# Rows of C by DMA instead of TensorE and ScalarE, and a rectifier moved from VectorE to ScalarE

## What is computed

```python
xz = x @ Win.T;  xi, z = xz[..., :256], silu(xz[..., 256:])
Bm, C = x @ WB.T, x @ WC.T                      # 16 values a token each
dt = softplus(x @ Wdt.T + bdt + dt_bias)
denom = 1 - dt * A * 0.5                        # A = -exp(A_log), 256 x 16
state[e, s] = (1 + dt*A*0.5) / denom * state[e, s] + dt / denom * Bm[s] * xi[e]
out[e] = sum_s state[e, s] * C[s]
y = layernorm(out * z) @ Wout.T
```

## Time and profile before

| | |
|---|---|
| median of 3 runs | 2897.46 us (2897.29 to 2911.29) |
| the profiled run | 2903.22 us, its span 2901.3 us |
| busy over the span | PE 2358.4 us (81%), DVE 1983.2 (68%), ACT 1950.0 (67%), POOL 1471.6 (51%) |
| state-space stage, 1279 to 2010 us | PE 509.56 us, DVE 658.89, ACT 538.78, POOL 538.20 of 731 |
| DVE in 40 slices | 2333367767767677458988989897776676767664 |
| DMA | 30.41 MB in the span, 3.5% of 16 engines |

### The profile page before, as it was taken

One profiled execution on the slowest core, in us unless ns is written; L12 is line 12 of the kernel. 1 busy time (PEld: TensorE's weight loads), 2 busy tenths in 40 slices (PEclk: granted clock), 3 DMA queues, 4 the chain that ended last, 5 costly groups with the idle time before them and its releaser, 6 DMA issues. The chain is left out here.

```text
span 2901.3 us, 47111 instructions
## 1 busy us (share of the span) xinstructions
PE 2358.4 (81%) x13516; PEld 1233.4 (43%) x13516; DVE 1983.2 (68%) x5318; ACT 1950.0 (67%) x4833; POOL 1471.6 (51%) x1308
## 2 busy tenths in 40 slices
PE   6999778888888888766766767776888888888887
PEld 3555445545555455422222222222454445544543
DVE  2333367767767677458988989897776676767664
ACT  3444357777777777567877677775777777776674
POOL 1222145545545555347776777774654554554442
PEclk9999879999999999978988888879999999999999
DMA  3000000000000000000000000000000000000000
GB/s 126 1 0 0 1 12 12 12 8 11 12 9 16 8 11 11 4 0 0 1 1 1 0 1 0 1 0 4 12 12 9 12 12 8 16 12 19 15 11 15
DMA packets 12195, 30.41 MB, mean 10 GB/s; under 512 B 2240, under 2 KB 2240, under 8 KB 11456
## 3 DMA queue, kind: packets, MB, share of 16 engines
q1 hardware_dynamic: 11968, 27.99, 3.5%
HBM read 9.11 MB, written 2.10 MB: 4 GB/s over the span
## 5 line engine op out<-in xcount | busy, mean ns | idle before, releaser
L500 POOL TENSOR_TENSOR arena<-arena 128x512 f32<-128x512 f32 x256 | 325.1, 1270 | 782.9 <-DVE arena L1469 782.9
L544 POOL TENSOR_TENSOR arena<-arena 128x512 f32<-128x512 f32 x256 | 328.8, 1301 | 128.5 <-ACT arena L1243 120.4
L1111 ACT ACTIVATE arena<-psum 128x512 f32<-128x512 f32 x256 | 152.6, 596 | 300.9 <-PE psum L824 300.5
L1475 DVE TENSOR_REDUCE SS<-arena 128x8 f32<-128x512 f32 x256 | 174.8, 683 | 259.3 <-ACT arena L1111 257.9
L824 PE MATMUL psum<-rest,HA 128*128 128x512 f32 x512 | 276.5, 623 | 51.1 <-DVE arena L1469 51.1
L513 POOL TENSOR_TENSOR P<-P,RS 128x512 f32<-128x512 f32 x256 | 266.5, 1041 | 93.8 <-DVE RS L1401 92.6
L1555 DVE TENSOR_TENSOR_SCAN arena<-arena,psum 128x512 f32<-128x512 f32 x256 | 310.9, 1215 | 3.2
L910 PE MATMUL psum<-BS,tabs 96*128 96x512 bf16 x384 | 146.7, 443 | 204.2 <-DVE arena L1555 202.4
L979 PE MATMUL psum<-arena,first 128*128 128x512 f32 x512 | 289.7, 655 | 10.9 <-POOL arena L535 10.6
L775 PE MATMUL psum<-HN,rest 128*128 128x512 f32 (+1 forms) x384 | 214.9, 674 | 98.9 <-ACT arena L1126 51.4
L506 POOL TENSOR_TENSOR arena<-arena,SC 128x512 f32<-128x512 f32 x256 | 273.1, 1067 | 29.8 <-DVE SC L1480 29.6
(11 more groups left out here) (222 smaller groups left out, 5878.9 us busy)
## 6 DMA issues: line engine op xcount, KB each, us to landing
arena<-arena SPq DMA_DIRECT2D x128, 128.0 KB, 2.3
rest<-in_rest SPq DMA_DIRECT2D x1, 4183.0 KB, 23.0
X<-in_x SPq DMA_DIRECT2D x1, 2048.0 KB, 11.0
out<-X SPq DMA_DIRECT2D x8, 256.0 KB, 2.4
first<-in_first SPq DMA_DIRECT2D x1, 1445.5 KB, 6.6
tabs<-in_tabs SPq DMA_DIRECT2D x1, 1216.0 KB, 13.5
```

The source lines that it names most:

```text
L500: nc.gpsimd.tensor_tensor(CQ[:, n % 2, :], CQ[:, n % 2, :], SQN[:, n % 2, :], ALU.add).then_inc(f_rope, 1)
L544: nc.gpsimd.tensor_tensor(WU[:, k % DEEP, :], RG[:, k % DEEP, :], U[t.j % 2][:, k % 2, :], ALU.mult).then_inc(m_wu, 1)
```

## The change

- The rows of C no longer go through TensorE and ACT. ACT copies the 32 rows of B and C from PSUM to a tile CF in SBUF (two deep) and rounds BS from CF. SP stores C's 16 rows of CF to DRAM (`c_rows`), waits for it, and loads each row back, repeated over 128 partitions, into CS, which is now four rows deep. A load waits for POOL's odd product four states back (`m_pco`); one semaphore for each of the four slots tells DVE and POOL that the row is there.
- DVE's even product reads CS instead of C_BANK; POOL's odd product reads CS as before.
- `spread_c` on TensorE and `copy_c` on ACT go.
- The positive part of v (PV) is made by ACT as a Relu with the bias, each half right behind its absolute value and ahead of the exponential, instead of by DVE.
- The first remainder (L1613) reads CF instead of SIDE; TensorE's later use of SIDE waits for CF.

```diff
@@ -283,20 +283,23 @@
         AB = shared("mamba", [128, DEEP, NT])
         WU = shared("mamba", [128, DEEP, NT])
         HS = shared("mamba", [128, DEEP, NT])
-        CS = shared("mamba", [128, 2, NT])
+        CS = shared("mamba", [128, 4, NT])
+        CF = [shared("mamba", [32, NT]) for k in range(2)]
         PC = shared("mamba", [128, DEEP, NT])
-        B_BANK, C_BANK, ACC_BANK = (bank[0], bank[2]), (bank[1], bank[3]), (bank[4], bank[5])
+        B_BANK, ACC_BANK = (bank[0], bank[2]), (bank[4], bank[5])
         SIDE = bank[6]
         STEPS = 2 * NS
-        m_bc = sem("m_bc")
+        m_cf = sem("m_cf")
+        m_cr = sem("m_cr")
+        c_rows = nc.dram_tensor("c_rows", (2, NS, NT), f32).ap()
-        m_cs = sem("m_cs")
+        m_cs = [sem(f"m_cs{k}") for k in range(4)]
@@ -471,8 +474,17 @@
                     k.wait_pair(f_x, -1)
                     sp_.dma_start(out[:, k.tokens(-1)], X[:, k.tokens(-1)]).then_inc(out_done, 16)
 
-            for ph in range(2):
-                passes(sp_, ph, sp_slot)
+            passes(sp_, 0, sp_slot)
+            for j in range(PAIRS):
+                for s in range(NS):
+                    if s == 0:
+                        sp_.wait_ge(m_cf, j + 1)
+                        sp_.dma_start(c_rows[j % 2, :, :], CF[j % 2][NS:2 * NS, :]).then_inc(m_cr, 16)
+                        sp_.wait_ge(m_cr, 16 * j + 16)
+                    if NS * j + s >= 4:
+                        sp_.wait_ge(m_pco, NS * j + s - 3)
+                    sp_.dma_start(CS[:, s % 4, :], c_rows[j % 2, s:s + 1, :].to_broadcast([128, NT])).then_inc(m_cs[s % 4], 16)
+            passes(sp_, 1, sp_slot)
             sp_.wait_ge(out_done, 16 * PAIRS)
 
 
@@ -529,10 +541,10 @@
             layers_pool(0)
             def odd_times_c(t, s):
                 k = 2 * s + 1
-                t.wait_ge(m_cs, NS, s + 1)
+                t.wait_ge(m_cs[s % 4], 64, 16 * (s // 4) + 16)
                 t.wait_ge(m_hs, STEPS, k + 1)
                 t.wait_ge(m_acc, STEPS, k + 1 - DEEP)
-                nc.gpsimd.tensor_tensor(PC[:, k % DEEP, :], HS[:, k % DEEP, :], CS[:, s % 2, :], ALU.mult).then_inc(m_pco, 1)
+                nc.gpsimd.tensor_tensor(PC[:, k % DEEP, :], HS[:, k % DEEP, :], CS[:, s % 4, :], ALU.mult).then_inc(m_pco, 1)
 
             def pool_turn(t):
                 for k in range(STEPS):
@@ -916,10 +928,6 @@
                     t.wait_ge(m_bs, 3, 3)
                 spread(t, k, k // 2, B_BANK[k % 2], m_bb)
 
-            def spread_c(t, s):
-                t.wait_ge(m_pce, NS, s - 1)
-                spread(t, s, NS + s, C_BANK[s % 2], m_bc)
-
             def half_sum(k, weight, source, done):
                 last = mm(STAT, weight(k), source[:, k, :], start=k == 0, stop=k == 1)
                 if k:
@@ -970,6 +978,7 @@
                 elif k in (20, 23):
                     half = (k - 20) // 3
                     t.wait_ge(m_zs if half else m_bd, 2, 1, pair=1)
+                    t.wait_ge(m_cf, 1, 1, pair=1)
                     mm(SIDE, W("b_win", 256 + 128 * half, 384 + 128 * half), HN[:, :], start=True, stop=True).then_inc(m_zp, 1)
 
             def accumulate(t, k):
@@ -984,15 +993,11 @@
             def pe_turn(t):
                 if t.states:
                     spread_b(t, 0)
-                    spread_c(t, 0)
                     spread_b(t, 1)
-                    spread_c(t, 1)
                 for k in range(STEPS):
                     if t.states:
                         if k + 2 < STEPS:
                             spread_b(t, k + 2)
-                        if k % 2 == 0 and 2 <= k < STEPS - 2:
-                            spread_c(t, k // 2 + 1)
                     if t.before:
                         pe_ending(t, k)
                     if t.after:
@@ -1198,6 +1203,7 @@
                     for half in range(2):
                         t.wait_ge(m_vp, 2, half + 1, pair=1)
                         A(AV[:, half, :], (SIDE, STAT)[half], ACT.Abs, bias=dt_bias_b[:, half:half + 1]).then_inc(m_abs, 1)
+                        A(PV[:, half, :], (SIDE, STAT)[half], ACT.Relu, bias=dt_bias_b[:, half:half + 1]).then_inc(m_max, 1)
                     t.wait_ge(m_abs, 2, 2, pair=1)
                     A(AV[:, :, :], AV[:, :, :], ACT.Exp, scale=-1.0).then_inc(m_exp, 1)
                     t.wait_ge(m_w, 1, 1, pair=1)
@@ -1210,8 +1216,10 @@
                 elif k == 21:
                     t.wait_ge(m_bp, 1, 1, pair=1)
                     t.wait_ge(m_bb, STEPS, STEPS, pair=-1)
-                    t.wait_ge(m_bc, NS, NS, pair=-1)
-                    A(BS[(t.j + 1) % 2][0:32, :], SIDE[0:32, :], ACT.Copy).then_inc(m_bs, 1)
+                    t.wait_ge(m_pco, NS, NS, pair=-1)
+                    A(CF[(t.j + 1) % 2][:, :], SIDE[0:32, :], ACT.Copy).then_inc(m_cf, 1)
+                    t.wait_ge(m_cf, 1, 1, pair=1)
+                    A(BS[(t.j + 1) % 2][0:32, :], CF[(t.j + 1) % 2][:, :], ACT.Copy).then_inc(m_bs, 1)
                 elif k in (23, 25):
                     part = (k - 21) // 2
                     t.wait_ge(m_bd, 2, part, pair=1)
@@ -1227,11 +1235,6 @@
                     A(LD[(t.j + 1) % 2][:, :, :], WV[:, :, :], ACT.Ln).then_inc(m_ld, 1)
                     nc.scalar.preload_act_table_set(SIG_TANH)
 
-            def copy_c(t, s):
-                t.wait_ge(m_bc, NS, s + 1)
-                t.wait_ge(m_pco, NS, s - 1)
-                A(CS[:, s % 2, :], C_BANK[s % 2], ACT.Copy).then_inc(m_cs, 1)
-
             def act_turn(t):
                 for k in range(STEPS):
                     if t.states:
@@ -1245,8 +1248,6 @@
                         A(AB[:, k % DEEP, :].rearrange("p (b t) -> p b t", b=2)[:, :, 1:],
                           d.rearrange("p (b t) -> p b t", b=2)[:, :, 1:], ACT.Tanh, bias=th_bias[:, c:c + 1],
                           scale=-0.5).then_inc(m_ab, 1)
-                        if k % 2 == 0 and k:
-                            copy_c(t, k // 2 - 1)
                     if k == 10:
                         nc.scalar.preload_act_table_set(EXP_LN)
                     if t.before:
@@ -1255,8 +1256,6 @@
                         act_beginning(t, k)
                     if k == 10:
                         nc.scalar.preload_act_table_set(SIG_TANH)
-                if t.states:
-                    copy_c(t, NS - 1)
 
             pairs(act, act_turn)
             nc.scalar.preload_act_table_set(EXP_LN)
@@ -1555,10 +1554,10 @@
                 v.tensor_tensor_scan(HS[:, k % DEEP, :], AB[:, k % DEEP, :], B_BANK[k % 2], 0.0, ALU.mult, ALU.add).then_inc(m_hs, 1)
 
             def times_c(t, k):
-                t.wait_ge(m_cs, NS, k // 2 + 1)
+                t.wait_ge(m_cs[k // 2 % 4], 64, 16 * (k // 8) + 16)
                 t.wait_ge(m_hs, STEPS, k + 1)
                 t.wait_ge(m_acc, STEPS, k + 1 - DEEP)
-                TT(PC[:, k % DEEP, :], HS[:, k % DEEP, :], C_BANK[k // 2 % 2], ALU.mult).then_inc(m_pce, 1)
+                TT(PC[:, k % DEEP, :], HS[:, k % DEEP, :], CS[:, k // 2 % 4, :], ALU.mult).then_inc(m_pce, 1)
 
             def dve_ending(t, k):
                 if k in (0, 1):
@@ -1598,9 +1597,6 @@
                     t.wait_ge(m_exp, 1, 1, pair=1)
                     t.wait_ge(m_ld, 1, 1)
                     TS(WV[:, :, :], AV[:, :, :], 1.0, None, ALU.add).then_inc(m_w, 1)
-                    for half in range(2):
-                        TS(PV[:, half, :], (SIDE, STAT)[half], dt_bias_b[:, half:half + 1], 0.0,
-                           ALU.add, ALU.max).then_inc(m_max, 1)
                 elif k == 13:
                     t.wait_ge(m_w, 1, 1, pair=1)
                     STT(AV[:, :, :], WV[:, :, :], -1.0, AV[:, :, :], ALU.add, ALU.subtract).then_inc(m_lost, 1)
@@ -1610,7 +1606,7 @@
                     t.wait_ge(m_bs, 3, part + 1, pair=1)
                     if part:
                         t.wait_ge(m_bd, 2, 1, pair=1)
-                    TT(BR[32 * part + 32:32 * part + 64, :], BR[32:64, :] if part else SIDE[0:32, :],
+                    TT(BR[32 * part + 32:32 * part + 64, :], BR[32:64, :] if part else CF[(t.j + 1) % 2][:, :],
                        bs[32 * part:32 * part + 32, :], ALU.subtract).then_inc(m_bd, 1)
                 elif k == 20:
                     t.wait_ge(m_dt, 1, 1, pair=1)
```

## The result

The changed kernel takes 2921.84 us in the median (2915.29 to 2923.41, 4 runs) for 2898.41 of the kernel before on the same occasions; the ratio is 1.0066, 95% interval [1.0034, 1.0099]. It is slower by some 19 us by the ratio and 23 by the medians: the sign and the place of the forecast were right, and its size, 2931 us, was 9 us too high. The profiled run has 2920.39 us and a span of 2918.6, 17.3 longer than before.

A forecast was written before the change was run, and what follows sets the result against it. DVE's queue in the state-space stage was taken to bound the kernel; 48.3 - 6.6 - 9.2 - 6.3 + 3.2 + 3 = +32.4 us on 2897.5 gave some 2930 (forecast 2931), range 2893 to 2985.

The forecast's parts named there:

- (a): DVE's 128 even products, now with two SBUF inputs, wait for the running POOL instruction: +48.3 us, bounds 0 and 151.
- (f): POOL is pushed back 0.45 us by each product it meets, and DVE waits on it: +3 us, bounds 0 and +15.
- (b): DVE's waits for ACT ahead of L1600 and L1596 absorb part of the products' added time: -6.6 us.
- (d): ACT's queue before the exponential loses copies of C and gains two Relus, so DVE waits less: -6.3 us, bounds 0 to -15.
- (c): L1602's two instructions leave DVE for ACT, 1.32 us in each of 7 pairs: -9.2 us.
- (e): ACT's extra copy costs 0, at most 5 us; the first L1613, now with two SBUF inputs, costs +3.2 us.
- (g): Spreading the rows of C by DMA, 2.4 to 3 us per row, stays hidden: 0.
- (h): TensorE loses 128 spreading matmuls: 0; a lower granted clock in the stage costs +3 us at most.
- the starved case: Rival: each product waits until POOL ends its lead, +196 us, 3090 with the rest; chance 0.07, in full or in part.

## Why the prediction was right, and where it wasn't

(a) **The products**: +44.0 us for +48.3. Of the 128, 96 took over 0.72 us, and where the timeline keeps POOL's instructions apart nearly all of these (73 of 81) end 0.5 to 0.6 us after one, as read from L1577. That the operand is the cause is shown from both sides: put in SBUF alone it makes the loss, put back in PSUM it takes the loss away. The changed kernel's product (ns min/median/max), and one plain cycle, DVE and POOL:

```profile
L1560 DVE TENSOR_TENSOR arena<-arena x128: 674/1014/1698, 1286.2 to 2014.0; 128x512 f32<-128x512 f32 x128
```

```profile
1986.38 1.22 DVE L1554 TENSOR_TENSOR_SCAN arena<-arena,psum 128x512 f32<-128x512 f32 x1
...
1987.12 2.93 POOL L556 TENSOR_TENSOR arena<-arena 128x512 f32<-128x512 f32 x2
...
1988.10 0.84 DVE L1560 TENSOR_TENSOR arena<-arena 128x512 f32<-128x512 f32 x1
...
1990.20 1.27 POOL L547 TENSOR_TENSOR arena<-arena 128x512 f32<-128x512 f32 x1
...
1990.69 1.22 DVE L1554 TENSOR_TENSOR_SCAN arena<-arena,psum 128x512 f32<-128x512 f32 x1
```

The cycle of two states is 1990.69 - 1986.38 = 4.31 us for 4.15, the product 0.84 us and POOL's pair (L556, L544 before) 2.93. Step (f) had worked out 4.33. The Trainium skill's rule (SBUF — State Buffer, "SBUF: two separate sides") agrees with these rows as far as the one running instruction goes: 1.70 us is the longest of the 128 products, so none was overtaken. It doesn't cover the 7.05 us above.

(b) and (d) **Waits for ACT**: -16.5 us in the two waits for the -12.9 worked out. The two steps don't add, though: the operand alone takes 12.1 us out of these waits (7.3 + 4.5 us for 23.9), where (b) had 6.6, and the DMA route alone 13.2, where (d) had 6.3 with the Relus in it. Either drains what the other would have saved, and that the sum came near is luck. ACT no longer waits for its copies; it now waits for the scan four steps back (us in total, times, longest), the bound named in (d):

```profile
ACT arena L1248 <- DVE arena L1554: 118.4, 98, 3.2
```

(c) **L1602**: the -9.2 us are in the sum, but the step was read too narrowly: it left out that DVE, earlier by as much, then waits for POOL at steps 17 and 19. This costs 7.9 us in the kernel before (13.4 for 5.5) and 8.9 in the changed one (9.5 for the 0.6 of the version with the positive part on DVE). The move's sign turns on what else meets POOL there: alone in the kernel before it costs 0.4%, in the changed kernel its undoing costs 13 us of stage, by the products of states 7 and 8.

(e) **The remainder from CF**: the first remainders took 1.14 us for 0.68, the +3.2 us worked out; the second ones gave back 0.8.

(f) **POOL pushed back**: the waits ahead of L1549 and of the scan grew by 10.1 us, I had 3, inside the bounds of 0 and 15. The reason given for them isn't borne out for the larger part: with the operand alone, where the products meet POOL too (+48.7 us), the wait for POOL ahead of L1549 falls from 15.7 to 11.0 us. It is the Relus that raise it, to 20.5.

(g) **DMA**: 3.1 us to landing for the 2.4 to 3 expected, hidden, with twice the loads too.

(h) **TensorE**: the granted clock went from 0.85 to 0.82 in the stage and DVE's wait for L910 from 14.9 us to 16.2. Nothing more.

In the rivals, the starved case comes to 3084 us by its own terms (2897.5 + 196 - 9.3), not 3090.

**The term that was mis-sized** is the one I left at zero in the sum and had only in the rivals: the other instructions that share the port. The clip went from five overtaken in seven to none, -17.3 us, while L1577 grew by 5.7. With these two terms, +32.4 would have been +20.8, and the stage shows +16.4. The starved rival is right as a mechanism, for both kinds of instruction, but struck none of the 128 products of this kernel. That the forecast of the time was only 9 us off owes something to luck: -17.3 and +7.1 (the waits of (f) beyond its 3) were not in it and have opposite signs.

**What stays open** is what decides whether a waiting DVE instruction gets the port after one POOL instruction or only when POOL pauses. The two cases of the earlier trace rows start alike, with the same POOL instructions around them to about 0.01 us, and end 3.7 us apart. It isn't the kind (the clip with two inputs) nor one instruction's place (the later clip). One pattern runs through all the profiles: in the four kernels with the product in SBUF (the changed one, the operand alone, two loads, the positive part on DVE again) the clip lasted 1.75 us in all 28 cases and nothing was overtaken; in each of the ten with the product in PSUM, 3 to 7 of 7 pairs had an instruction overtaken. So the -17.3 us came with the operand. Why is open, and I have no experiment that makes one given instruction overtaken or not. Among kernels with the product in PSUM, whatever shifts the order of DVE and POOL can change the count, at 3.7 to 5.9 us each; as each kernel was profiled once, how much the count varies from one execution to the next isn't known.

## What to carry to other kernels

Before an operand moves from PSUM to SBUF, see what the other input is and what GpSimd does meanwhile: a DVE product with two SBUF inputs waited here for the GpSimd instruction that was running and so lasted up to 2.88 us, and the same product with one input in PSUM lasted 670 to 690 ns in 128 of 128 cases. Take a producer's relief and a consumer's operand as two edits; here the one alone was worth -16.8 us of the stage and the other +23.2, and both together +29.6, not +6.4, as both draw on the same waits. Before work is moved off the busiest engine, see whom that engine waits for next: of the 9.2 us taken from DVE 8 to 9 came back as wait for GpSimd. And when an edit shifts two engines that share a port, compare the durations of all instructions that use it, not only of the one that was edited.

## What was unexpected of the hardware

A DVE instruction that waits for the port can be passed by several GpSimd instructions in a row: 5.27 us for an instruction of 0.69 that takes 1.6 when it waits for one, 5.8 for one of 1.27, 4.6 and 7.05 for remainders of 0.68. In the cases shown it ends when GpSimd runs out of work: behind the 7.05 us, GpSimd stood idle for 2.03 us. The clip was struck in 0 to 7 of 7 pairs, and moving it away handed this to the second remainder, the next instruction that needs the port. While the 128 products used the port too, it struck nothing.
